# Retention with batches 1 to 15 in a five-fold loop of three turns, and projections that run two batches past the last

## What is computed

```python
def retention(x, Wqk, bqk, Wv, bv, Wn, bn, Wo, bo):      # x: normalised, 16 x 256 x 128
    qk = x @ Wqk + bqk; v = x @ Wv + bv; n = x @ Wn + bn   # 16 heads of 8
    q, k = qk.reshape(b, s, 2, 16, 8)[:, :, 0], ...[:, :, 1]
    scores = einsum('bthd,bshd->bhts', q, k)
    attn = scores * tril(ones((s, s))) / exp(n)[..., None]
    ctx = einsum('bhts,bshd->bthd', attn, v)
    return ctx.reshape(b, s, 128) @ Wo + bo
```

## Time and profile before

| | us |
|---|---|
| median of three runs | 1843.05 (1841.29 to 1848.9) |
| span of the profiled execution, first to last instruction | 1846.8 |
| time of the profiled execution outside its span | not shown |
| PE busy (share of the span) | 1709.5 (93%) |
| ACT busy | 1462.7 (79%) |
| DVE busy | 1022.5 (55%) |
| POOL busy | 453.3 (25%) |
| granted TensorE clock, mean | 0.974 |

### The profile page before, as it was taken

The page is one execution under the profiler, slowest core; times in us unless marked ns, Lnnn a source line. Parts: engine busy times, 40 slices in busy tenths (PEclk is TensorE's granted clock), DMA queues, the critical chain, the costliest instruction groups (busy, mean ns, idle before and its releaser), DMA issues. The chain is left out here.

```text
span 1846.8 us, 67972 instructions
## 1 busy us (share of the span) xinstructions
PE 1709.5 (93%) x27988; PEld 1024.6 (55%) x27988; DVE 1022.5 (55%) x3242; ACT 1462.7 (79%) x2635; POOL 453.3 (25%) x385
## 2 busy tenths in 40 slices
PE   7898799999998999999999978999989879999888
PEld 4675455555554555555555435566663346666633
DVE  5454633334332333443333059999975489999854
ACT  4342599999998999999999948999973379999932
POOL 1113100000000000000000037777730176777400
PEclk9897899999999999999999989999999999999999
DMA  1000211111111111111110031111110001111100
GB/s 60 3 1 26 106 48 50 62 44 62 62 53 45 50 53 53 62 62 49 55 37 31 3 109 27 24 34 34 29 27 11 1 18 33 32 26 31 32 15 34
DMA packets 47439, 73.56 MB, mean 40 GB/s; under 512 B 8400, under 2 KB 38224, under 8 KB 47184
## 3 DMA queue, kind: packets, MB, share of 16 engines
q1 hardware_dynamic: 47184, 69.85, 12.2%
HBM read 21.08 MB, written 2.10 MB: 13 GB/s over the span
## 5 line engine op out<-in xcount | busy, mean ns | idle before, releaser
L689 ACT ACTIVATE x_probs<-x_pss 128x1024 f32<-128x1024 f32 x832 | 806.6, 1021 | 54.3 <-PE x_pss L610 39.6
L624 PE MATMUL x_acc<-x_probs,x_v 128*32 128x256 f32 x6656 | 438.6, 381 | 0.0
L610 PE MATMUL x_pss<-x_qx,x_kx 32*128 32x256 bf16 x9984 | 350.0, 271 | 12.9 <-issue 5.8
L610 PEld LDWEIGHTS x_pss<-x_qx,x_kx 32*128 32x128 bf16 x9984 | 222.2, 93 | 199.9 <-ACT x_probs L689 180.5
L624 PEld LDWEIGHTS x_acc<-x_probs,x_v 128*32 128x32 f32 x6656 | 206.9, 110 | 93.5 <-issue 9.5
L1291 ACT ACTIVATE l_prob<-l_sim,l_neg_top,l_inv_norm 128x128 f32<-128x128 f32 x512 | 245.7, 487 | 4.4 <-DVE l_neg_top L1185 4.4
L736 DVE COPY x_vnext<-x_psp 128x128 f32<-128x128 f32 (+1 forms) x199 | 59.3, 298 | 316.7 <-PE x_psp L588 312.2
L917 POOL TENSOR_TENSOR l_turned_half<-l_raw,l_tabB 128x512 f32<-128x512 f32 x128 | 182.0, 1443 | 60.1 <-ACT l_raw L1250 59.8
L665 POOL COPY x_zq<-zT 128x256 f32 (+1 forms) x15 | 6.0, 402 | 763.1 <-PE x_psp L595 693.5
L927 POOL TENSOR_TENSOR l_direct<-l_direct,l_turned_half 128x1024 f32<-128x1024 f32 x64 | 155.6, 2432 | 0.0
L1177 DVE CUSTOM_DVE_ANT_0 l_sim<-l_pss,w_window 128x128 f32<-128x128 f32 x512 | 117.7, 285 | 3.6 <-issue 2.2
(11 more groups left out here) (185 smaller groups left out, 2642.8 us busy)
## 6 DMA issues: line engine op xcount, KB each, us to landing
x_kx<-x_kp SPq DMA_DIRECT2D x96, 208.0 KB, 2.4
x_cT<-in_context SPq DMA_DIRECT2D x16, 832.0 KB, 4.8
x_qx<-x_qp SPq DMA_DIRECT2D x48, 192.0 KB, 3.2
l_vmid<-l_vt SPq DMA_DIRECT2D x64, 128.0 KB, 2.3
xT<-in_x SPq DMA_DIRECT2D x8, 256.0 KB, 4.4
shifted<-zT SPq DMA_DIRECT2D x32, 64.0 KB, 2.0
hs<-zT SPq DMA_DIRECT2D x32, 64.0 KB, 2.0
out_x<-xT SPq DMA_DIRECT2D x8, 256.0 KB, 2.0
```

The lines of the kernel that those rows point to most:

```text
L610: ins = pe.matmul(pss[bank(k, 2 * p + r // 2)][:, r % 2, e, :], kx[par][rows, g, j * P:(j + 1) * P], qx[par][rows, g, a * S:(a + 1) * S], ...
L624: ins = pe.matmul(acc[32 * r:32 * r + 32, 0:S], v[:, j, g, r, :], probs[SLOT[p]][r // 2][:, r % 2, e, :], start=(u == 0), stop=(u == UNITS ...
L689: act.activation(probs[SLOT[p]][y][:, :, :, :], pss[bank(k, 2 * p + y)][:, :, :, :], ACT.Sigmoid, scale=HD ** -0.5).then_inc(weighed, 1)
```

## The change

The turns of PE, ACT and DVE become one written out and a loop of five rounds with three turns (15 divided by NB). With that the helper left goes, so that turns 14 and 15 also run project, tokens, queries, keys, inverse and split_queries, for batches 16 and 17 that don't exist. What these compute is used by nobody. GpSimd keeps the old shape of three turns, a loop of three rounds and four turns; its turns 13 and 14 now also stage batches 16 and 17, from a copy of the input of batch 15.

```diff
-        def left(n):
-            return not isinstance(n, int) or n < B
-
         def turns(eng, body):
-            for n in range(3):
-                body(n, n % NB)
-            with eng.Fori(0, 3) as i:
+            body(0, 0)
+            with eng.Fori(0, (B - 1) // NB) as i:
                 for u in range(NB):
-                    body(3 * i + 3 + u, u)
-            for n in range(12, B):
-                body(n, n % NB)
+                    body(NB * i + 1 + u, (1 + u) % NB)
...
             def mix(n, u):
                 pe.wait_ge(state_ready, n + 1)
-                if left(n + 2):
-                    pe.wait_ge(k_ready, n + 3)
+                pe.wait_ge(k_ready, n + 3)
...
                 sum_states(n, u)
-                if left(n + 2):
-                    project(n + 2, (u + 2) % NB)
+                project(n + 2, (u + 2) % NB)
                 mix(n, u)
...
             def turn(n, u):
-                if left(n + 2):
-                    keys(n + 2, (u + 2) % NB)
-                    inverse(n + 2, (u + 2) % NB)
+                keys(n + 2, (u + 2) % NB)
+                inverse(n + 2, (u + 2) % NB)
                 take_out(n)
-                if left(n + 2):
-                    split_queries(n + 2, (u + 2) % NB)
+                split_queries(n + 2, (u + 2) % NB)
...
-                if left(n + 2):
-                    tokens(n + 2, (u + 2) % NB)
-                    queries(n + 2, (u + 2) % NB)
+                tokens(n + 2, (u + 2) % NB)
+                queries(n + 2, (u + 2) % NB)
...
             def stage(n, u):
                 if past(n, NB):
                     pool.wait_ge(kv_projected, n - NB + 1)
-                pool.tensor_copy(staged[u][:, :], zT[:, ds(n * S, S)]).then_inc(z_staged, 1)
+                from_batch = min(n, B - 1) if isinstance(n, int) else n
+                pool.tensor_copy(staged[u][:, :], zT[:, ds(from_batch * S, S)]).then_inc(z_staged, 1)
...
-                if left(n + 3):
+                if not isinstance(n, int) or n + 3 < B + 2:
                     stage(n + 3, u)
...
-            turns(pool, turn)
+            for n in range(NB):
+                turn(n, n)
+            with pool.Fori(0, 3) as i:
+                for u in range(NB):
+                    turn(NB * i + NB + u, u)
+            for n in range(4 * NB, B):
+                turn(n, n % NB)
```

## The result

| | before | after |
|---|---|---|
| median, us | 1843.05 (1838.87 to 1853.05, 13 runs) | 1852.92 (1848.77 to 1856.35, 13 runs) |
| ratio, 95% interval | | 1.0044 (1.0029 to 1.006) |
| span of the profiled execution | 1846.8 | 1847.5 |

The forecast was 1824. The kernel is 0.44% slower, within the 0.5% that I called no change and far outside my range.

The account below looks back on a forecast made before the run. PE was taken to bound a retention turn that runs well, with late new code stalling it elsewhere. Savings of 18.94 + 0.15 - 0.12 = 19.0 us off the 1843.05 median gave 1824, range 1818 to 1831.

Parts of the forecast that it names:

- the turns of the new loop: Retention, first mask of turn 3 to that of turn 15: 81.84 us where 100.78 stood, 18.94 saved.
- turn 3: Retention, end of the loop's first round: 7.01 us instead of 8.72, a 2.05 stall gone, 0.34 added for the way back.
- Turns 1 and 2: Retention, the new loop's first two turns: code still met for the first time, so 8.35 and 9.13 us kept.
- first rival: Retention: turns 1 to 3 as dear as the old first round, 29.65 us against 24.49; total 1829.2; chance 0.12.
- second rival: Retention: each of four ways back fetches its target, 2.33 us each, 9.3 given back; total 1833.3; chance 0.03.
- third rival: Retention's loop needs one piece of code more than is kept, every round streams; 17.7 us slower, 1860.8; chance 0.02.
- The end of the stage: Retention, from turn 15's first mask to ACT's last split copies: 7.71 us instead of 7.86, 0.15 less.
- the 9.93: Retention, turns 12 to 14: 20.47 us instead of 30.40 as repeated code, 9.93 saved.
- Norm n2: Stage after retention, inherits the clock: between 3.1 us gained and 2.0 lost, taken as 0.
- sentence on later stages: All stages after retention shift in the code; a stall is worth 1.4 to 2.3 us; taken as 0, one or two either way.
- fourth rival: Stages after retention: four more exposed stalls of 2.33 us, 9.3 given back; total 1833.3; chance 0.05.
- The rule quoted in the prediction: Skill page: a taken branch outside a small window must fetch code again, unroll; set aside for two packet-free ways back, 0.34 us.

## Why the prediction was wrong

**What held.** Of the sum's terms: the turns of the new loop 81.96 us against 81.84; turn 3, where I moved the one stall, 7.08 against 7.01. A stall was paid there in three variants of the changed kernel with filler, though, where turn 3 took 10.08, 10.08 and 10.45 us, 3.0 to 3.4 more and not the 2.05 that I kept in the range. Turns 1 and 2 took 8.97 and 9.40 where I kept 8.35 and 9.13, 0.9 more. Turns 1 to 3 thus cost 25.4 us and not the first rival's 29.65. The second rival (each way back fetches) is refuted for PE's loop by the empty DMA view, the third (PE's loop streams) likewise. The end of the stage took 7.70 us from the first mask of turn 15 to ACT's last split copies (142.08 to 149.78) against 7.71. From the first mask of turn 0 to the end of the stage, which is what the sum counts, retention gained 17.8 us (132.61 to 114.85) against the forecast of 19.0: turns 0 to 2 took 1.2 more, the rest came as summed. That the windows view gives 19.1 is a matter of where it ends the stage. The size is in part luck as well: the 9.93 that I took for turns 12 to 14 rests on the slowest of four executions of the old loop on PE, which took 30.4, 25.4, 23.3 and 22.4 us, and against the second profile of the kernel before the stage's gain by the windows view is 15.2 instead of 19.1. In whole-kernel times the versions without the loss are 14 to 22 us (0.77 to 1.18%) faster than the kernel before.

**Norm n2.** I had left it between a gain of 3.1 and a loss of 2.0 and taken 0. It took 26.9 us both times when counted from PE's last work in retention; from its own first projection it took 24.4 (150.10 to 174.5) instead of 25.7 (166.99 to 192.7), 1.3 less. The pause came as expected and with it a low clock, though for 3.4 us only: the first three projections began at 150.10 and took 4.51 us, against 5.46 in the earlier trace rows.

```profile
150.10 4.51 PE L112 MATMUL n_wide<-zT,r_wo 128*128 128x512 f32 x6 [2.46 <-PEq L221]
```

**The step that failed** is the sentence on later stages: that all of them shift their place in the code, that a stall is worth 1.4 to 2.3 us, and that I take 0 with one or two stalls either way. The shift was seen, its kind was not. I thought of straight code, where a shift moves a stall, and not of the loops further on, where it can turn every round from kept to fetched. It cost 22.4 us in the first local attention instead of 0. Of that, 16.2 stand in the second and third rounds (6.4 and 9.8), 5.2 before the first round ends, 1.0 behind the loop. My fourth rival had the right place and a price of 9.3, and a chance of 0.05. My third rival had the mechanism that the runs speak for, a loop cut into one piece more than is kept, but I weighed it for the edited loop on PE alone, and the earlier trace rows spoke for that loop only. Two things were to be had from the trace of before: that rounds two and three of the local attention bring in hardly any code, so that there was something to lose; and that DVE has 2.75 us of slack in a round of 67.5, so that a late fetch of its would be on the path. The median came out 29 us above the 1824. Of what is left beside the 22.4, 1.2 are turns 0 to 2 of retention and 3.5 the two feed-forwards, whose reason is open; the times of single executions spread by more than the rest.

**The rule quoted in the prediction.** The Trainium skill, page "Runtime: NRT & Kernel Launch", section "Instruction fetch mechanics", warns that a branch to code outside a small window of pages costs a fetch. I set it aside on the strength of the earlier trace rows. The trace agrees with it where the loop no longer fits: 5 or 6 packets of 8 KB in a round of 322 instructions for DVE, and 10 us. Where the loop fits, the trace shows none. As the rule speaks only of targets outside the window, did not show its opposite, as I wrote, but a loop that it doesn't concern. The page gives blocks of 256 instructions; here the loss repeats after 128 (rounds of 76.2 and 77.4 us with a shift of 128) and DVE's and ACT's code comes in packets of 8 KB, and the measurement decides.

**What stays open.** The medians differ by 9.9 us and the ratio by 0.44%, some 8 us, but the two profiled spans by 0.7 only. Cross attention and norm n3, 5.5 and 1.6 us shorter in this one profile of the changed kernel, account for most of that; that they do so by chance is argued from their spread over the other profiles, not shown. Why the two feed-forwards take 83 to 87 us in different profiles was not followed up.

## What to carry to other kernels

A loop body that fits on chip is a property of its place as well as of its length. When an edit changes the number of instructions on an engine, look at every later loop of that engine: does its second round fetch code today, and has the engine slack in it? If it fetches nothing and the engine has little slack, the edit may cost its whole gain there, and a handful of met waits ahead of the loop may be worth 20 us. Read instruction packets by round, not "issue" time alone: ACT's loop fetched as much as DVE's, with 0.4 us of "issue" in a round of 67.5, and cost nothing.

## What the runs showed of the hardware

- DVE's loop of 322 instructions was kept with its first instruction at 1219, 1238, 1240 and 1242 and, in the second local attention, 1856, 1875, 1894, 1896, 1898, 1984 and 2112, and lost at 1200, 1328 and 1456. Modulo 128 that is 64 to 106 kept and 48 lost; the numbers are those of the compiled program without its labels, and what stands ahead of it on the chip is not known. ACT's loop of 291 was kept at 1227, 1230 and 1239 and lost at 1191.
- A lost loop fetched five or six packets of 8 KB in a round, per engine, all on queue 14. PE's code came in packets of 16 KB on queue 8; its loop of 1128 instructions was kept in every variant.
- A loop that fetches on DVE costs more than the gaps in which it waits for code: DVE's busy time rose from 64.75 to 70.69 us in a round, in operations that each ran beside one of POOL (2.12 us for 0.16). The kernel before has one of them in a round (1.75 us for 0.69), with no code on its way.
